# Cross-attention: the scores as two 64-row tiles of TensorE's array, the values and the turned output as two 64-column tiles

## The reference, cut to what matters

```
q = (layernorm(x) @ Wq + bq)   -> 16 heads x 32 queries x 16 channels, for each of 64 batches
k = ctx @ Wk + bk, v = ctx @ Wv + bv   -> 16 heads x 257 keys x 16 channels
attn = softmax(clip(q @ k.T * 16 ** -0.5, -10000, 10000))
x = x + (attn @ v) @ Wo + bo
```

## Time and profile before

| | |
|---|---|
| median of 3 runs | 1191.21 us (1185.65 to 1194.63) |
| span of the profiled execution | 1183.4 us |
| PE, share of the span | 90% |
| PEld | 82% |
| DVE | 68% |
| POOL | 62% |
| ACT | 55% |
| granted TensorE clock, mean | 0.954 |

### The profile page before, as it was taken

One profiled execution on the slowest core, in us unless ns is written; L12 is line 12 of the kernel. 1 busy time (PEld: TensorE's weight loads), 2 busy tenths in 40 slices (PEclk: granted clock), 3 DMA queues, 4 the chain that ended last, 5 costly groups with the idle time before them and its releaser, 6 DMA issues. The chain is left out here.

```text
span 1183.4 us, 27537 instructions
## 1 busy us (share of the span) xinstructions
PE 1070.7 (90%) x8152; PEld 967.4 (82%) x8153; DVE 804.4 (68%) x2353; ACT 654.9 (55%) x1517; POOL 738.6 (62%) x813
## 2 busy tenths in 40 slices
PE   5899999999999999779799963899999735999998
PEld 3799999999999999668678852788888633998897
DVE  7566666666666666665466658976766575787784
ACT  3556555655555555163377858666666463544551
POOL 2687777777777778234588931877767403655533
PEclk9999999999999999889999985999999966999999
DMA  5211111122112211179000041233333246835600
GB/s 155 72 55 53 56 55 53 53 62 67 53 53 64 62 55 48 31 216 374 21 1 0 1 90 68 41 50 51 52 53 54 36 157 208 234 104 141 172 6 10
DMA packets 68549, 94.30 MB, mean 80 GB/s; under 512 B 12764, under 2 KB 48048, under 8 KB 68496
## 3 DMA queue, kind: packets, MB, share of 16 engines
q1 hardware_dynamic: 52464, 73.03, 19.3%
q0 software_dynamic: 16032, 20.62, 10.7%
HBM read 73.69 MB, written 22.18 MB: 81 GB/s over the span
## 5 line engine op out<-in xcount | busy, mean ns | idle before, releaser
L1916 POOL DMA_INDIRECT e_x<-rows,source x71 | 75.8, 1068 | 101.3 <-DVEq L1753 36.0
L122 POOL TENSOR_TENSOR xa_qbd<-qs,xw_c_mask8s 128x512 fp32r<-128x512 f32 x128 | 131.5, 1048 | 6.1 <-POOLq L133 3.8
L511 PE MATMUL xa_ob<-xa_v,xa_pT 128*128 128x65 f32 x1024 | 133.4, 273 | 0.2 <-DVE xa_pT L702 0.2
L632 ACT ACTIVATE xa_kT<-xa_kvp,xw_bk 128x258 fp32r<-128x258 f32 x128 | 60.8, 476 | 127.9 <-PE xa_kvp L465 120.7
L649 ACT ACTIVATE xa_pr<-xa_pr,xa_nm 128x257 f32<-128x257 f32 x256 | 109.6, 499 | 35.2 <-DVE xa_nm L698 35.1
L511 PEld LDWEIGHTS xa_ob<-xa_v,xa_pT 128*128 128x128 f32 x1024 | 124.8, 192 | 0.3 <-DVE xa_pT L702 0.3
L691 DVE TENSOR_SCALAR_CACHE_REDUCE xa_pr<-xa_sc 128x257 f32<-128x257 f32 x256 | 98.0, 421 | 22.4 <-PE xa_sc L491 22.4
L1927 POOL DMA_INDIRECT out_x<-e_y,target x32 | 54.2, 1693 | 74.5 <-DVE e_y L2714 63.4
L594 POOL TENSOR_TENSOR xa_ol<-xa_om,xa_tl 128x256 f32<-128x256 f32 x64 | 47.1, 736 | 78.7 <-DVE xa_rinv L719 78.5
L2551 PE MATMUL e_hb<-e_xTs,e_w1s 128*128 128x512 f32 x384 | 92.0, 400 | 1.9 <-issue 1.9
L2605 ACT ACTIVATE e_h<-e_hb,rc_F_b 128x512 f32<-128x512 f32 x64 | 44.1, 688 | 88.3 <-PE e_hb L2551 88.3
(11 more groups left out here) (369 smaller groups left out, 3265.8 us busy)
## 6 DMA issues: line engine op xcount, KB each, us to landing
e_w<-in_F_W SPq DMA_DIRECT2D x16, 1024.0 KB, 9.0
w<-in_W SPq DMA_DIRECT2D x24, 512.0 KB, 10.4
xa_ctx<-in_ctxT SPq DMA_DIRECT2D x32, 257.0 KB, 3.1
xa_ctx<-in_ctxT SPq DMA_DIRECT2D x64, 128.5 KB, 3.2
xa_vb<-vlx SPq DMA_DIRECT2D x64, 128.0 KB
rows<-xs_oT SPq DMA_DIRECT2D x4, 516.0 KB, 10.2
xs_oT<-in_x SPq DMA_DIRECT2D x4, 512.0 KB, 5.0
base<-xs_oT SPq DMA_DIRECT2D x4, 512.0 KB, 3.1
```

The costliest lines, as they stand in the source:

```text
L122: pool.tensor_tensor(dst, src, msk, ALU.mult).then_inc(o["q_ready"], 1)
L511: mm = pe.matmul(ob[:, 65 * g:65 * g + 65], pT[:, par, g, t, :], v[:, vs, t, g, :], start=(g == 0 and t == 0), stop=(g == G - 1 and t == 1 ...
L1916: return pool.indirect_dma_start(out=out, out_offset=None, in_=rows, in_offset=bass.IndirectOffsetOnAxis(ap=index, axis=0))
```

## The change

- `qbd` holds, for each h, one block of 128 columns, with both groups of the half in it: the four heads of group 2h on partitions 0 to 63, those of group 2h+1 on partitions 64 to 127. The mask is `c_mask4s`, and each of POOL's two operations in a step is 128x256, not 128x512.
- S issues its 12 matmuls with 64 rows each, the two groups of a half in turn: rows 0 to 63 write the bank of group 2h, rows 64 to 127 that of group 2h+1.
- `v` is held for two pairs of heads j, each with 32 channels and a column of ones (33 columns). V issues 16 matmuls (8 before), with 64 weight columns and 33 moving columns each, to partitions 0 to 63 and 64 to 127 of the output in turn.
- TO issues four matmuls (two before), with 64 weight columns each.
- DVE's `mask_output` reads 32 channels of a group twice (by a broadcast) where it read 64; its output is 128x256 as before. ACT's `store_v` writes the new layout, as many elements as before.

```diff
 def spread_queries(pool, o, w, qs, b, par):
-    msk = w["c_mask8s"][:].unsqueeze(1).unsqueeze(3).to_broadcast([P, 2, 8, L])
+    msk = w["c_mask4s"][:].unsqueeze(1).unsqueeze(3).to_broadcast([P, 2, 4, L])
     for a in range(2):
-        src = qs[:, a, :, bass.ds(b * L, L)].unsqueeze(2).to_broadcast([P, 2, 8, L])
-        dst = o["qbd"][:, par, a].rearrange("p (h j) (e q) -> p h (j e) q", h=2, q=L)
+        src = qs[:, a, :, bass.ds(b * L, L)].unsqueeze(2).to_broadcast([P, 2, 4, L])
+        dst = o["qbd"][:, par, a].rearrange("p h (e q) -> p h e q", q=L)
...
-                    for g in (2 * h, 2 * h + 1):
-                        out = sc[:, g, 0:SE]
-                        pe.matmul(out, qbd[:, par, 0, g, :], kT[:, par, 0, h, :], start=True, stop=False)
-                        pe.matmul(out, qbd[:, par, 0, g, :], kT[:, par, 1, h, :], start=False, stop=False)
-                        mm = pe.matmul(out, qbd[:, par, 1, g, :], kT[:, par, 0, h, :], start=False, stop=True)
+                    for n, (a, c) in enumerate(((0, 0), (0, 1), (1, 0))):
+                        for j in range(2):
+                            rows = slice(64 * j, 64 * j + 64)
+                            mm = pe.matmul(sc[:, 2 * h + j, 0:SE], qbd[rows, par, a, h, :], kT[rows, par, c, h, :],
+                                           start=(n == 0), stop=(n == 2))
...
-                        mm = pe.matmul(ob[:, 65 * g:65 * g + 65], pT[:, par, g, t, :], v[:, vs, t, g, :],
-                                       start=(g == 0 and t == 0), stop=(g == G - 1 and t == 1), skip_group_check=True)
+                        for j in range(2):
+                            mm = pe.matmul(ob[64 * j:64 * j + 64, 33 * g:33 * g + 33], pT[:, par, g, t, 64 * j:64 * j + 64],
+                                           v[:, vs, t, g, j, :], start=(g == 0 and t == 0),
+                                           stop=(g == G - 1 and t == 1), skip_group_check=True)
...
-                    mm = pe.matmul(ob[:, OT + L * h:OT + L * h + L], on[:, P * h:P * h + P], istack[:],
-                                   start=True, stop=True, skip_group_check=True)
+                    for c in (0, 64):
+                        mm = pe.matmul(ob[c:c + 64, OT + L * h:OT + L * h + L], on[:, P * h + c:P * h + c + 64], istack[:],
+                                       start=True, stop=True, skip_group_check=True)
...
-                act.activation(v[:, vs, :, :, 0:64], kvp[:, par, :].rearrange("p (t g c) -> p t g c", t=2, g=G),
-                               ACT.Copy).then_inc(v_ready, 1)
+                act.activation(v[:, vs, :, :, :, 0:32].rearrange("p t g j c -> p (t g j) c"),
+                               kvp[:, par, :].rearrange("p (n c) -> p n c", c=32), ACT.Copy).then_inc(v_ready, 1)
...
-                dve.tensor_tensor(total[:, par, :], o[:, :, 64], plast[:, par, :], ALU.add).then_inc(total_ready, 1)
-                dve.tensor_tensor(om[:, par, :].rearrange("p (g c) -> p g c", g=G), o[:, :, 0:64],
-                                  mask64[:].unsqueeze(1).to_broadcast([P, G, 64]), ALU.mult).then_inc(om_ready, 1)
+                dve.tensor_tensor(total[:, par, :], o[:, :, 32], plast[:, par, :], ALU.add).then_inc(total_ready, 1)
+                dve.tensor_tensor(om[:, par, :].rearrange("p (g j c) -> p g j c", g=G, j=2),
+                                  o[:, :, 0:32].unsqueeze(2).to_broadcast([P, G, 2, 32]),
+                                  mask64[:].rearrange("p (j c) -> p j c", j=2).unsqueeze(1).to_broadcast([P, G, 2, 32]),
+                                  ALU.mult).then_inc(om_ready, 1)
```

More of the change, by code:

```diff
@@ L102, in cross_attention_opening @@
          "ctx": m.sb("xa_ctx", [P, 2, 2, 2, S]), "cs": m.sb("xa_cs", [P, 2, 2, 2, SE], F32R),
-         "v": m.sb("xa_v", [P, 4, 2, G, 65]), "qbd": m.sb("xa_qbd", [P, 2, 2, G, P], F32R)}
+         "v": m.sb("xa_v", [P, 4, 2, G, 2, 33]), "qbd": m.sb("xa_qbd", [P, 2, 2, 2, P], F32R)}
     for name in "eps_set rows_zeroed ones_ready pad_ready wh_ready wl_ready ch_pad_ready ch_ready cr_ready q_ready".split():
@@ L182, in _ @@
             for i in range(4):
-                pool.memset(o["v"][:, i, :, :, 64], 1.0).then_inc(o["ones_ready"], 1)
+                pool.memset(o["v"][:, i, :, :, :, 32], 1.0).then_inc(o["ones_ready"], 1)
             pool.memset(o["pad"][:], 0.0).then_inc(o["pad_ready"], 1)
@@ L329, in cross_attention_weights @@
               (lambda t: t[0:64, 1, :], io[name][P:DC, :]), (lambda t: t[64:P, 1, :], io[name][P:DC, :]))
-    for name, shape in (("bk", [P, 2]), ("c_ident", [P, P]), ("c_istack", [P, L]), ("c_mask8s", [P, 8]),
+    for name, shape in (("bk", [P, 2]), ("c_ident", [P, P]), ("c_istack", [P, L]), ("c_mask4s", [P, 4]),
                         ("c_mask64", [P, 64])):
@@ L351, in cross_attention_phase @@
         wk, wv, bk, bo, cl = w["Wk"], w["Wv"], w["bk"], w["bo"], w["ctx_last"]
-        ident, istack, mask8, mask64, maskj = w["c_ident"], w["c_istack"], w["c_mask8s"], w["c_mask64"], w["c_maskj"]
+        ident, istack, mask64, maskj = w["c_ident"], w["c_istack"], w["c_mask64"], w["c_maskj"]
         wks, wvs, ctx, cs, v, qbd = [o[n] for n in ("wks", "wvs", "ctx", "cs", "v", "qbd")]
@@ L706, in mask_output @@
                 dve.wait_ge(o_ready, b + 1)
-                o = ob[:, 0:G * 65].rearrange("p (g c) -> p g c", g=G)
+                o = ob[:, 0:G * 33].rearrange("p (g c) -> p g c", g=G)
                 dve.wait_ge(plast_ready, b + 1)
@@ L773, in constants @@
         "c_mask8": (p[:, None] // HD == np.arange(8)).astype(np.float32),
-        "c_mask8s": -SCALE * (p[:, None] // HD == np.arange(8)).astype(np.float32),
+        "c_mask4s": -SCALE * (p[:, None] % 64 // HD == np.arange(4)).astype(np.float32),
         "c_mask64": (p[:, None] // L == np.arange(64) // HD).astype(np.float32),
```

## The result

The changed kernel takes 1131.89 us (median of 4 runs, 1129.98 to 1139.23) against 1190.43 for the kernel before (4 runs): ratio 0.952, 95% interval 0.948 to 0.956, so 4.4 to 5.2% faster, 58.5 us. The forecast was 1120, the range 1103 to 1167.

The account below looks back on a forecast made before the run. PE was taken to bound the cross-attention: 0.72 + 0.78 + 0.13 - 0.50 = 1.13 us saved a step, 72 us over 64 steps. Span 1111 plus 7.8 gave 1119, say 1120 us; 8-in-10 range 1103 to 1167.

Parts of the forecast that it names:

- the band of 1105 to 1132: Whole kernel's time in us if the forecast holds; given a chance of 0.57.
- What bounds the kernel: Cross-attention: PE sets the 6.93 us step, others wait for it; a us saved on its line counts 64 times.
- S: Scores matmuls in cross-attention: two row tiles run side by side, 1.52 us becomes 0.80, saving 0.72 a step.
- Rival 1: Scores: row tiles don't overlap and stay at 1.52 us; 26 us saved, 1165 us; chance 0.19 for 1150 to 1175.
- The full-array price that stood beside the column tiles: L1335 against L1312: a full-array matmul takes at least 0.24 us, column-tile records under 0.067, so tiles stream together.
- V and TO: Values and turned output: records at 0.029 us each; values save 0.78 us a step, turned output 0.13.
- Rival 3: Values and turned output: short records don't get cheaper; step 1.85 us longer, 1309 us; chance 0.01.
- Nothing else is late: Other engines at a 5.80 us step: all in time, thinnest margin 0.35 us for `rest_k`; DVE's wait near 1 us.
- all of the 1.13: PE's saving per step in us; taken off DVE's 1.90 us wait, it leaves about 0.8.
- the switches: Five tile changes in each cross-attention step: 0.50 us lost, between 0.42 if costs coincide and 0.60 if they add.
- 64 full steps were charged: Cross-attention phase: 64 steps, each saving 1.13 us, make 72 us.
- 7.8 us were put between span and median: Whole kernel: the median lies 7.8 us over the span, so a span of 1111 gives 1119, say 1120 us.

Follow-up runs that it names:

- `pool_double`: Changed kernel with each of POOL's two query operations in a step preceded by a copy of itself into an unread buffer; 1133.01 us, ratio 0.953.
- `same_tile`: Changed kernel with all twelve scores matmuls of a step on rows 0 to 63, same amount of work; 1177.58 us, ratio 0.990 to the kernel before.
- `two_more_switches`: Changed kernel with the turned output issued in the middle of the value projection, seven tile changes a step, not five; 1152.82 us, ratio 0.967.
- `no_loop`: Changed kernel with the 64 steps of TensorE, DVE, ACT and POOL written out, without a loop; 1125.96 us, ratio 0.945.
- `scores_one_tile`: Changed kernel issuing in each half the three scores matmuls of rows 0 to 63 first, then those of rows 64 to 127; 1134.02 us, ratio 0.951.
- `values_only`: Changed kernel with scores and spread queries put back as before; values and turned output stay in 64-column tiles; 1166.66 us, ratio 0.979.
- `scores_only`: Kernel before with only the scores in two 64-row tiles and the queries spread for that; 1167.31 us, ratio 0.980.

## Why the prediction was right, and which terms were mis-sized

The mechanism held, and the sum was 12 us too hopeful: 1131.89 is at the very edge of the band of 1105 to 1132 that it called its forecast. Right, by its own steps:
- *What bounds the kernel.* PE's line. A saving on PE appears in the time (57 us over the phase), one on POOL doesn't (`pool_double`).
- *S.* Six pairs, 0.80 us plus a switch: 0.92 measured. Rival 1 (no overlap) was the right rival to keep: `same_tile` is that case, and costs 45.7 us over the changed kernel, near the 0.71 x 64 = 45 of its expectation. It takes 1178 us and not rival 1's 1165, by about the same 12 us that the forecast lacks. The full-array price that stood beside the column tiles, 0.24 us for L1335, was read the wrong way round: with the switch behind it included it is the most that such a record takes, not the least. Against 0.067 that changes nothing.
- *V and TO.* 0.029 us a record, taken from L1346, held for the new shape: (0.64 - 0.224) / 15 = 0.028 in V0. Rival 3 is gone with it: the warning of the Trainium skill's "TensorEngine Tiling (Array Packing)", section "Instruction Overhead", against taking the tiling factor from a small dimension doesn't come true here. A likely reason is that the moving side was not what a record cost. With 65 columns moving it was 0.107 us, with the scores' 258 only 0.119, both with 128 weight columns, whose load the profile gives 0.19 us, and one of 64 columns 0.14. TO moves 32 columns before and after, and its record went from 0.09 us (0.36 / 4) to 0.03 (0.25 / 8). But 64 columns and a second tile beside them come together in every run, so what each is worth isn't shown.
- *Nothing else is late.* PE has no wait on another engine. `rest_k` ends 3.38 us after S's start (409.15 + 0.48 = 409.63), forecast near 3.5; the projection starts at 3.96, so the margin is 0.58 us and not 0.35. DVE's wait for L512 is 1.59 us in this step and not near 1. The prediction took all of the 1.13 from the wait of 1.90, although by its own account 0.44 of DVE's other waits go first: 1.90 + 0.44 - 1.13 is 1.2. The step is 0.12 longer than forecast, and `bounds` (L698, now L701) is followed by the next operation 0.07 us after its start where it was 0.32, which makes up the rest; why it is shorter isn't shown by any run.

The term that was mis-sized is the switches: 0.50 us a step was taken, between 0.42 (a switch hides the change of type) and 0.60 (they add). They add. From the parts of the step after: into the scores 0.13, from the scores to T0 0.12 and another 0.05 on T0's own records, to the turned output 0.09, to the projection 0.11, from it to V1 0.11, 0.61 in all and, by itself, `two_more_switches` puts one at 0.10. That is 0.11 x 64 = 7 us too little. Two things were in no term. One is the turn of the loop, 0.07 us a step in the mean, 4 us, which was no cost before the change (the four steps of a round were 6.85, 6.93, 6.94 and 7.00, mean 6.93, as long as those outside the loop). The other is the phase's ends: 64 full steps were charged, but the steps there leave parts out. From the first L714 to the last there are 63 distances, for which the forecast's 1.13 gives 71 us, and 57.0 were saved. The 52 in the middle are 10 us short, by switches and turns, the 11 at the ends 4 us. With the 2 us of the lower clock that is more than the 12 us that the medians show; the rest lies within what runs differ by (the ratio's interval is about 10 us wide).

One base of the forecast can be split now: 7.8 us were put between span and median as what lies around the span and what runs differ by. The runs of the changed kernel give the first part: 1139.23 with a span of 1137.4, 1130.54 with 1128.8. It is 1.8 us; 1183.4 + 1.8 = 1185.2, so the profiled execution was about as fast as the fastest of the three (1185.65), and the other 6 us are spread. That does the forecast no harm: it is 1191 less 72 whichever way they split.

## What to carry to other kernels

When small matmuls use half of the array, look in the same trace for any group that runs in tiles already and take its start-to-start distance as the price; a record's own duration says nothing. Price each change of the tile, about 0.1 us here, on top of the change between fp32r and fp32, and count them around the step: two half-array parts that stand next to each other share one. And when a change gives the bounding engine more instructions in a step, look at the turn of the loop: it was free at 60 matmul records in a step and cost up to 0.2 us at 80. Where the code is short enough to write out, that is worth a run (`no_loop`, 1126 us, is the fastest kernel here).

## What the runs showed of the hardware that had not been expected

- Matmuls of two row tiles run beside each other even when three of one tile stand in the program ahead of three of the other (`scores_one_tile`: the same 0.92 us for S as in turn). On one tile they take 1.62 us.
- In a loop of four steps the turn costs 0.1 and 0.2 us in two of the four, in the kernels with 80 matmul records in a step (`values_only`, `same_tile`, the changed kernel), and nothing in those with 60 (the kernel before, `scores_only`). A loop of 28 costs 4.9 us at its one turn, 1.4 of it by the lower clock after 3.5 us in which PE stood; straight code of 64 steps costs nothing that a step's length shows.
- The granted clock fell to its 1.2 GHz level at the phase's start in all eight profiles of kernels with the full change and a loop, and in none of the other four, after the same matmuls. The cause is open.
- No run here has the value projection in 64-column tiles, which would take two of the five switches away without moving anything. Its fp32r matmuls would have to run in that mode, and no row here shows one that does.
